# Sandwich layer on eight cores: LayerNorm sums through an accumulator output, one residual add on GpSimd, one PSUM copy on ScalarE

## The chip, the cores and the metric

One Trainium2 chip, all 8 cores, one program with different data on each core. The metric is device time in microseconds (us) of the slowest core. Engines are called PE (TensorE), DVE (VectorE), ACT (ScalarE), POOL (GpSimd) and SP (SyncE, which here only issues DMAs).

## What is computed

Input x is (2, 4096, 4096) float32. Each core has 1024 consecutive tokens of it (plus one neighbour row on each side for the convolution). Cut to what matters:

```python
def ln(x):   # no scale or shift; the last one of the layer has gamma and beta
    return (x - mean(x)) / sqrt(var(x) + 1e-5)

def attn(t1):
    c = conv1d(t1, conv_w, width 3, 4096 -> 3072) + conv_b
    q, k, v = split(c)                       # blocks of 128 tokens, 16 heads of 64
    o = softmax(causal(q wq . k wk / 8)) (v wv)
    return (o wo + bo) @ proj_w + proj_b      # -> a, (tokens, 4096)

def ffn(t2):
    h   = relu(t2 @ up_w) ** 2                 # 4096 -> 8192
    moe = (t2 @ fc1_w @ expert_w) * sum(top2(t2 @ gate_w))
    return ln(h @ down_w + moe @ fc2_w) * gamma + beta

x2  = x + ln(attn(ln(x)))
out = x2 + ln(ffn(ln(x2)))
```

## The kernel before

All weights stream from HBM; the matmuls use bf16. The work of a core goes through stages one after the other:

1. **First stage (lines 322 to 384), called A here.** 8 tiles of 128 tokens x 4096, then a ninth tile that holds the two halo rows. SP loads a tile of x (line 353). `ln_stats` (line 308) makes mean and 1/sigma: DVE sums the tile (`reduce_sum`), ACT squares it with an accumulator output beside that, then follow three DVE operations on one column and Ln and Exp on ACT. DVE normalizes to bf16 (line 360). `tm_to_fm` transposes in 8 groups: PE writes 4 transposes to one of two PSUM banks, DVE copies the group out (line 340), so that tokens lie along the columns.
2. Convolution (line 420), q, k and v, attention, output projections (line 670). The last one leaves the result feature-major in `a_fm`.
3. **Stage between projection and feed-forward (lines 692 to 765), called F here**, again 8 tiles of 128 tokens x 4096, one after the other:
   - SP loads x (line 706). PE transposes `a_fm` back in 8 groups (line 714), DVE copies each out to `atm` in bf16 (line 719).
   - `ln_stats` on `atm`, then DVE normalizes into `x2t`, float32 (line 729), and adds x in place (line 731). SP stores `x2t` (line 736).
   - `ln_stats` on `x2t`, DVE normalizes to `t2s`, bf16 (line 741). PE transposes (line 752), DVE copies to `stage` (line 756), SP stores it (line 761).
4. Feed-forward in two halves of 512 tokens; behind each half the final LayerNorm and the second residual add.

The work of each engine runs in the order in which the program is written. There is no scheduler: every wait is on a counting semaphore, and an engine that waits holds all that is behind it. SV counts DVE's operations, SC ACT's, SP (the semaphore) PE's groups, SX0 and SX1 loads of x, SS0 and SS1 stores. Each DVE and ACT operation goes through a wrapper (`EngWrap`) that first waits for the engine's own operation before, so all of them carry line 175. Three points on the order in stage F:

- The load of x for tile t+1 stands in SP's queue behind the store of tile t's `stage`, which waits for the last copy of tile t:

```python
        p.wait(sy, "SV", c_stage)                     # line 760, tile t
        ins = sy.dma_start(dt2sp[t], ...)
        p.wait(sy, "SV", xin_free[par])               # line 705, tile t+1
        c_load = p.inc(sy.dma_start(xinF[par], ...), f"SX{par}", 16)
```

- DVE waits for that load ahead of the sum over `atm` (line 722), though the sum does not read x.
- `stage` lies on `x2t`, so PE waits for the store of `x2t` (line 745) ahead of the second set of transposes.

Of the kernel before, what the change touches and what calls it, by code (L numbers as in the profile page):

```python
# [9 lines left out]
AF = mybir.ActivationFunctionType  # L10
ALU = mybir.AluOpType
# [4 lines left out]
D = 4096  # L16
# [11 lines left out]
EPS = 1e-5  # L28
# [98 lines left out]
class P:  # L127

    def __init__(self, nc):
        self.nc = nc  # L130
        self.sems = {}
        self.cnt = {}
        self._auto = set()
        names = ["SA", "SP", "SV", "SC", "SX0", "SX1", "SS0", "SS1",
                 "WQ", "WK", "WV", "WO"] + [f"D{i}" for i in range(5)]
        for name in names:
            self.sems[name] = nc.alloc_semaphore(name=name)
            self.cnt[name] = 0
# [44 lines left out]
def build(taps=(), stop_phase=99):  # L183
    nc = bass.Bass("TRN2", target_bir_lowering=False)
    p = P(nc)
    te, sy, po = nc.tensor, nc.sync, nc.gpsimd
    ve = EngWrap(p, nc.vector, "SV")
    se = EngWrap(p, nc.scalar, "SC")
# [65 lines left out]
    def stat(i):  # L254
        return stats[:, i : i + 1]
# [47 lines left out]
    def tap_barrier():  # L303
        if dtaps:
            for q in (te, sy, po, nc.vector, nc.scalar):
                p.wait(q, "SA")

    def ln_stats(src, sq_trash, width=D):
        p.inc(ve.reduce_sum(stat(S_SUM), src, axis=AX.X), "SV")
        ia = se.activation(sq_trash, src, AF.Square, accum_out=stat(S_SQ))  # L310
        c_sq = p.inc(ia, "SC")
        ve.tensor_scalar(stat(S_MU), stat(S_SUM), 1.0 / width, None, ALU.mult)
        p.wait(ve, "SC", c_sq)
        ve.tensor_tensor(stat(S_VAR), stat(S_MU), stat(S_MU), ALU.mult)
# [12 lines left out]
    t1s_free = [0, 0]
    tb_free = [0, 0]
# [15 lines left out]
    for t in range(NT + 1):  # L344
        par = t % 2
        if t == NT:
            p.wait(ve, "SV", xin_free[par])
            c = p.inc(ve.memset(xin[par], 0.0), "SV")
            p.wait(sy, "SV", c)
            ins = sy.dma_start(xin[par][0:2], dxh)  # L350
        else:
            p.wait(sy, "SV", xin_free[par])
            ins = sy.dma_start(xin[par], dx[t * 128 : (t + 1) * 128])
        c_load = p.inc(ins, f"SX{par}", 16)
        p.wait(ve, f"SX{par}", c_load)
        p.wait(se, f"SX{par}", c_load)
        p.wait(se, "SP", t1s_free[par])
        c_r = ln_stats(xin[par], t1s[par])
        p.wait(ve, "SC", c_r)
        iv = ve.tensor_scalar(t1s[par], xin[par], stat(S_MU), stat(S_R),  # L360
                              ALU.subtract, ALU.mult)
        c_n = p.inc(iv, "SV")
        xin_free[par] = c_n
        p.wait(te, "SV", c_n)
        if t < NT:
            tm_to_fm(t1s[par],
                     [t1T3[:, g * 4 : g * 4 + 4, 1 + t * 128 : 1 + (t + 1) * 128]
                      for g in range(8)])
        else:
            for g in range(8):  # L370
                tb = 4 + (g % 2)
                p.wait(te, "SV", tb_free[g % 2])
                for j in range(4):
                    ch = g * 4 + j
                    it = te.transpose(pbb[tb][:, j * 128 : (j + 1) * 128],
                                      t1s[par][:, ch * 128 : (ch + 1) * 128], id_bf)
                c = p.inc(it, "SP")
                p.wait(ve, "SP", c)
                src3 = pbb[tb].rearrange("p (a b) -> p a b", a=8)
                ve.tensor_copy(t1T3[:, g * 4 : g * 4 + 4, 0:1], src3[:, 0:4, 0:1])  # L380
                iv = ve.tensor_copy(t1T3[:, g * 4 : g * 4 + 4, 1025:1026], src3[:, 0:4, 1:2])
                tb_free[g % 2] = p.inc(iv, "SV")
        t1s_free[par] = p.cnt["SP"]
# [318 lines left out]
    p.wait(te, "SC", a_ready)  # L702
    for t in range(NT):
        par = t % 2
        p.wait(sy, "SV", xin_free[par])
        c_load = p.inc(sy.dma_start(xinF[par], dx[t * 128 : (t + 1) * 128]), f"SX{par}", 16)
        atm3 = atm[par].rearrange("p (a b) -> p a b", a=DC)
        p.wait(te, "SV", atm_free[par])
        for g in range(8):
            tb = 4 + (g % 2)  # L710
            p.wait(te, "SV", tb_free[g % 2])
            for j in range(4):
                m = g * 4 + j
                it = te.transpose(pbb[tb][:, j * 128 : (j + 1) * 128],  # L714
                                  a_fm[:, m * 1024 + t * 128 : m * 1024 + (t + 1) * 128],
                                  id_bf)
            c = p.inc(it, "SP")
            p.wait(ve, "SP", c)
            iv = ve.tensor_copy(atm3[:, g * 4 : g * 4 + 4],
                                pbb[tb].rearrange("p (a b) -> p a b", a=8)[:, 0:4])  # L720
            tb_free[g % 2] = p.inc(iv, "SV")
        p.wait(ve, f"SX{par}", c_load)
        p.wait(se, f"SS{par}", x2_spilled[par])
        p.wait(se, "SV", tb_free[0])
        p.wait(se, "SV", tb_free[1])
        c_r = ln_stats(atm[par], x2t[par])
        p.wait(ve, "SC", c_r)
        p.wait(ve, f"SS{par}", x2_spilled[par])
        ve.tensor_scalar(x2t[par], atm[par], stat(S_MU), stat(S_R),
                         ALU.subtract, ALU.mult)  # L730
        iv = ve.tensor_tensor(x2t[par], x2t[par], xinF[par], ALU.add)
        c_x2 = p.inc(iv, "SV")
        xin_free[par] = c_x2
        atm_free[par] = c_x2
        p.wait(sy, "SV", c_x2)
        c_spill = p.inc(sy.dma_start(dx2sp[t], x2t[par]), f"SS{par}", 16)
        p.wait(se, "SV", c_x2)
        p.wait(se, f"SS{par}", t2s_free[par])
        c_r2 = ln_stats(x2t[par], t2s[par])
        p.wait(ve, "SC", c_r2)  # L740
        iv = ve.tensor_scalar(t2s[par], x2t[par], stat(S_MU), stat(S_R),
                              ALU.subtract, ALU.mult)
        c_t2 = p.inc(iv, "SV")
        p.wait(te, "SV", c_t2)
        p.wait(te, f"SS{par}", c_spill)
        st3 = stage[par].rearrange("p (a b) -> p a b", a=DC)
        for g in range(8):
            tb = 4 + (g % 2)
            p.wait(te, "SV", tb_free[g % 2])
# [12 lines left out]
        t2s_free[par] = p.inc(ins, f"SS{par}", 16)
        x2_spilled[par] = t2s_free[par]
# [417 lines left out]
```

How the kernel before makes its waits and increments, by code:

```python
    def inc(self, instr, sem, n=1):  # L140
        if isinstance(instr, _Auto):
            return self.cnt[sem]
        instr.then_inc(self.sems[sem], n)
        self.cnt[sem] += n
        return self.cnt[sem]
# [1 line left out]
    def wait(self, eng, sem, val=None):  # L147
        v = self.cnt[sem] if val is None else val
        if v > 0:
            eng.wait_ge(self.sems[sem], v)
# [15 lines left out]
    def wait_ge(self, sem, v):  # L166
        return self._e.wait_ge(sem, v)
# [5 lines left out]
        def wrapped(*a, **k):  # L173
            p.wait(eng, semname)
            instr = fn(*a, **k)
            instr.then_inc(p.sems[semname], 1)
            p.cnt[semname] += 1
            return _Auto(instr)
```

## Time and profile before

| | us |
|---|---|
| two executions | 5212.37 and 4887.19, median 5049.78 |
| the profiled execution | 4884.38 |
| its span, first to last instruction, slowest core (core 3) | 4883.3 |
| spans of the eight cores | 4848.7 to 4883.3 |
| PE busy in the span | 3832.8 (78%) |
| DVE busy | 839.1 (17%) |
| ACT busy | 474.3 (10%) |
| POOL busy | 212.7 (4%) |

The profile is of the profiled execution on its slowest core. Busy shares are means over stages with different limits; what a stage waits for is read from its own stretch of the timeline and from the chain of waits that ended last. POOL is busy only with issuing DMAs.

### The profile page before, as it was taken

How to read it: one execution, taken by the hardware profiler on the slowest of the kernel's cores; microseconds unless marked ns; L12 is line 12 of the kernel's file. 1: busy time of each engine (PE TensorE's matmuls, PEld its weight loads, DVE VectorE, ACT ScalarE, POOL GpSimd, SP SyncE). 2: the span in 40 equal slices, each digit the busy share in tenths (PEclk: the TensorE clock that was granted, in tenths of full speed). 3: DMA queues.
4: the chain of work that ended last, by engine and by line, in shares of the span. 5: the costliest groups of instructions: out<-in, count | busy, mean ns of one | idle time of the engine just before them, and what ended most of it. 6: DMA issues, size and time to landing. Idle time of an engine off the chain costs nothing.

```text
span 4883.3 us, 43161 instructions; the slowest of 8 cores (4848.7 to 4883.3 us)
## 1 busy us (share of the span) xinstructions
PE 3832.8 (78%) x18161; PEld 1739.4 (36%) x18161; DVE 839.1 (17%) x1060; ACT 474.3 (10%) x621; POOL 212.7 (4%) x385
## 2 busy tenths in 40 slices
PE   1599999999648323879998999970779998999960
PEld 1244444444224111334443444430334443444430
DVE  4300000000360565110000000027110000000027
ACT  2100000002213221001111000001001111000001
POOL 0000000000001000000000000000000000000000
PEclk9999999999759655899999999985899999999985
DMA  6144444446004334568887777763569997777743
GB/s 157 38 75 75 75 76 78 78 78 104 0 1 60 113 129 150 101 114 153 152 152 137 142 134 140 144 128 117 112 122 151 154 153 137 134 140 143 139 91 116
DMA packets 76779, 548.38 MB, mean 112 GB/s; under 512 B 7529, under 2 KB 7977, under 8 KB 30506
## 3 DMA queue, kind: packets, MB, share of 16 engines
q0 software_dynamic: 64592, 444.69, 53.1%
q1 hardware_dynamic: 11998, 100.94, 5.8%
q8 instruction: 147, 2.41, 0.2%
q14 instruction: 42, 0.34, 0.0%
HBM read 948.32 MB, written 41.94 MB: 203 GB/s over the span
## 4 chain that ended last, share of the span: by engine, by line
PE 73%; DVE 13%; DMA 9%; issue 3%; SPq 1%; ACT 1%; DVEq 0%; ACTq 0%; POOL 0%; POOLq 0%
PE ps L902 21%; PE ps L420 20%; PE ps L1057 18%; DVE pool L175 13%; PE ps L995 5%; DMA pool<-fc1w 2%; PE ps L670 2%; DMA pool<-x 2%; PE ps L957 2%; DMA pool<-x2sp 1%; PE ps L489 1%; DMA pool<-expw 1%; SPq L831 1%; DMA pool<-fc2w 1%; ACT pool L175 1%
## 5 line engine op out<-in xcount | busy, mean ns | idle before, releaser
L902 PE MATMUL ps<-pool 128*128 128x512 bf16 x5120 | 1127.4, 383 | 55.0 <-DMA pool<-fc1w 36.2
L420 PE MATMUL ps<-pool 128*128 128x512 bf16 x4608 | 998.3, 379 | 0.9 <-DVE pool L175 0.9
L1057 PE MATMUL ps<-pool 128*128 128x512 bf16 x4096 | 899.4, 380 | 41.3 <-DMA pool<-fc2w 41.2
L902 PEld LDWEIGHTS ps<-pool 128*128 128x128 bf16 x5120 | 503.7, 99 | 680.7 <-issue 93.3
L175 DVE CAST pool<-ps 128x512 bf16<-128x512 f32 (+1 forms) x192 | 107.2, 558 | 3340.9 <-PE ps L995 1988.9
L420 PEld LDWEIGHTS ps<-pool 128*128 128x128 bf16 x4608 | 445.4, 97 | 553.6 <-issue 3.9
L1057 PEld LDWEIGHTS ps<-pool 128*128 128x128 bf16 x4096 | 397.4, 98 | 521.2 <-issue 49.4
L175 ACT ACTIVATE pool<-pool 128x512 bf16<-128x512 f32 (+5 forms) x259 | 260.9, 1007 | 1967.5 <-DVE pool L175 1934.1
L175 ACT ACTIVATE pool<-ps,pool 128x512 bf16<-128x512 f32 (+1 forms) x192 | 131.9, 687 | 1127.6 <-PE ps L420 975.1
L175 DVE TENSOR_REDUCE pool<-pool 128x1 f32<-128x4096 f32 (+2 forms) x73 | 220.3, 3018 | 81.7 <-DMA pool<-x 55.1
L995 PE MATMUL ps<-pool 128*128 128x512 bf16 x1024 | 231.5, 379 | 0.0
L752 PE MATMUL ps<-pool 128*128 128x128 bf16 x256 | 34.9, 302 | 234.6 <-DVE pool L175 234.6
L175 DVE COPY pool<-ps 128x128 bf16<-128x128 bf16 (+6 forms) x489 | 156.7, 320 | 328.1 <-PE ps L714 147.5
L175 DVE TENSOR_TENSOR pool<-pool 128x1 f32<-128x1 f32 (+3 forms) x106 | 188.5, 1779 | 63.5 <-DMA pool<-x2sp 52.5
L175 ACT ACTIVATE pool<-ps 128x512 f32<-128x512 f32 x128 | 76.4, 597 | 1246.7 <-PE ps L902 1246.7
L995 PEld LDWEIGHTS ps<-pool 128*128 128x128 bf16 x1024 | 100.1, 98 | 120.9
L957 PE MATMUL ps<-pool 128*128 128x512 bf16 x512 | 117.3, 391 | 21.9 <-DMA pool<-expw 19.4
L175 DVE TENSOR_SCALAR pool<-pool 128x1 f32<-128x1 f32 (+3 forms) x139 | 118.0, 849 | 46.6 <-ACT pool L175 35.8
L670 PE MATMUL ps<-pool 128*128 128x512 bf16 x512 | 113.5, 386 | 5.5 <-DMA pool<-projw 5.5
L867 PE MATMUL ps<-pool 128*1 128x128 f32 x8 | 3.0, 372 | 141.3 <-DVE pool L175 141.3
L752 PEld LDWEIGHTS ps<-pool 128*128 128x128 bf16 x256 | 22.9, 130 | 246.6 <-issue 246.6
L336 PE MATMUL ps<-pool 128*128 128x128 bf16 x256 | 35.0, 302 | 90.8 <-DVE pool L175 90.8
(59 smaller groups left out, 833.9 us busy)
## 6 DMA issues: line engine op xcount, KB each, us to landing
pool<-upw POOLq DMA_DIRECT2D x128, 1024.0 KB, 10.1
pool<-downw POOLq DMA_DIRECT2D x64, 2048.0 KB, 15.4
pool<-wconv POOLq DMA_DIRECT2D x72, 1024.0 KB, 16.4
pool<-x SPq DMA_DIRECT2D x16, 2048.0 KB, 10.9
pool<-fc1w POOLq DMA_DIRECT2D x32, 1024.0 KB, 9.3
pool<-fc2w POOLq DMA_DIRECT2D x32, 1024.0 KB, 19.4
x2sp<-pool SPq DMA_DIRECT2D x8, 2048.0 KB, 6.3
pool<-expw POOLq DMA_DIRECT2D x16, 1024.0 KB, 9.7
```

The lines of the kernel that those rows point to most:

```text
L175: instr = fn(*a, **k)
L336: it = te.transpose(pbb[tb][:, j * 128 : (j + 1) * 128], src_bf[:, ch * 128 : (ch + 1) * 128], id_bf)
L420: it = te.matmul(pbf[bk], sl[:, k * 128 : (k + 1) * 128], t1T[:, k * 1026 + base : k * 1026 + base + 512], start=(dw == 0 and k == 0), sto ...
L489: it = te.matmul(pbf[bk], w_sb[:, k * 1024 + pr * 128 : k * 1024 + (pr + 1) * 128], c_fm[:, (which * 8 + k) * 1024 + half * 512 : (which * ...
L670: it = te.matmul(pbf[bk], proj_sl[s][:, k * 128 : (k + 1) * 128], attnW[:, k * 1024 + half * 512 : k * 1024 + half * 512 + 512], start=(k ...
L752: it = te.transpose(pbb[tb][:, j * 128 : (j + 1) * 128], t2s[par][:, ch * 128 : (ch + 1) * 128], id_bf)
L831: ins = sy.dma_start(t2h3[:, :, tl * 128 : (tl + 1) * 128], dt2sp[half * 4 + tl])
L867: it = te.transpose(pbf[2][0:1, tl * 128 : (tl + 1) * 128], stat(S_RW), id_f32)
L902: it = te.matmul(pbf[bk], slots[s][:, k * 128 : (k + 1) * 128], rhs_fn(k), start=(k == 0), stop=(k == n_k - 1))
L957: it = te.matmul(pbf[bk], exp_sl[s][:, (j * LATC + k) * 128 : (j * LATC + k + 1) * 128], lat[:, k * 512 : (k + 1) * 512], start=(k == 0), ...
L995: it = te.matmul(pbf[bk], f2_sl[s][:, (j * LATC + k) * 128 : (j * LATC + k + 1) * 128], moe[:, k * 512 : (k + 1) * 512], start=False, stop ...
L1057: te.matmul(pbf[bk], dw_sl[s][:, k * 128 : (k + 1) * 128], hup[:, k * 512 : (k + 1) * 512], start=(k == 0), stop=False)
```

## The change

It has three parts, and the final LayerNorms keep the old `ln_stats`.

1. A new `ln_stats_fast` stands beside `ln_stats`. Instead of `reduce_sum`, DVE runs a `tensor_scalar` (times 1, plus 0) that writes the whole tile as float32 into a scratch area and puts the sum into `stat(S_SUM)` through the accumulator output. Stage A (9 calls) and stage F (16 calls) use it.
2. In stage F the 8 PSUM groups of the `a_fm` transposes are copied to `atm` by ACT (Identity) and no longer by DVE. PE waits for both kinds of copy (semaphores SC and SV) before each set of 8 groups.
3. In stage F the add `x2t + x` moves from DVE to POOL. A new semaphore SG carries its end to SP, PE, ACT and DVE.

```diff
+    def ln_stats_fast(src, sq_trash, sum_trash, width=D):
+        iv = ve.tensor_scalar(sum_trash, src, 1.0, 0.0, ALU.mult, ALU.add,
+                              accum_out=stat(S_SUM))
+        p.inc(iv, "SV")
+        ia = se.activation(sq_trash, src, AF.Square, accum_out=stat(S_SQ))
...
     def ln_stats(src, sq_trash, width=D):
         p.inc(ve.reduce_sum(stat(S_SUM), src, axis=AX.X), "SV")
...
-        c_r = ln_stats(xin[par], t1s[par])
+        c_r = ln_stats_fast(xin[par], t1s[par], trashA)
...
-        p.wait(te, "SV", atm_free[par])
+        p.wait(te, "SG", atm_free[par])
+        p.wait(te, "SV", tb_free2[0])
+        p.wait(te, "SV", tb_free2[1])
         for g in range(8):
             tb = 4 + (g % 2)
-            p.wait(te, "SV", tb_free[g % 2])
+            p.wait(te, "SC", af[g % 2])
...
-            p.wait(ve, "SP", c)
-            iv = ve.tensor_copy(atm3[:, g * 4 : g * 4 + 4],
-                                pbb[tb].rearrange("p (a b) -> p a b", a=8)[:, 0:4])
-            tb_free[g % 2] = p.inc(iv, "SV")
+            p.wait(se, "SP", c)
+            ia = se.activation(atm3[:, g * 4 : g * 4 + 4],
+                               pbb[tb].rearrange("p (a b) -> p a b", a=8)[:, 0:4],
+                               AF.Identity)
+            af[g % 2] = p.inc(ia, "SC")
         p.wait(ve, f"SX{par}", c_load)
         p.wait(se, f"SS{par}", x2_spilled[par])
-        p.wait(se, "SV", tb_free[0])
-        p.wait(se, "SV", tb_free[1])
-        c_r = ln_stats(atm[par], x2t[par])
+        p.wait(ve, "SC", af[0])
+        p.wait(ve, "SC", af[1])
+        c_r = ln_stats_fast(atm[par], x2t[par], trashF)
         p.wait(ve, "SC", c_r)
         p.wait(ve, f"SS{par}", x2_spilled[par])
-        ve.tensor_scalar(x2t[par], atm[par], stat(S_MU), stat(S_R),
-                         ALU.subtract, ALU.mult)
-        iv = ve.tensor_tensor(x2t[par], x2t[par], xinF[par], ALU.add)
-        c_x2 = p.inc(iv, "SV")
+        iv = ve.tensor_scalar(x2t[par], atm[par], stat(S_MU), stat(S_R),
+                              ALU.subtract, ALU.mult)
+        c_g = p.inc(iv, "SV")
+        p.wait(po, "SV", c_g)
+        p.wait(po, f"SX{par}", c_load)
+        it = po.tensor_tensor(x2t[par], x2t[par], xinF[par], ALU.add)
+        c_x2 = p.inc(it, "SG")
...
-        p.wait(sy, "SV", c_x2)
+        p.wait(sy, "SG", c_x2)
         c_spill = p.inc(sy.dma_start(dx2sp[t], x2t[par]), f"SS{par}", 16)
-        p.wait(se, "SV", c_x2)
+        p.wait(se, "SG", c_x2)
+        p.wait(ve, "SG", c_x2)
         p.wait(se, f"SS{par}", t2s_free[par])
-        c_r2 = ln_stats(x2t[par], t2s[par])
+        c_r2 = ln_stats_fast(x2t[par], t2s[par], trashF)
...
+        p.wait(te, "SC", af[0])
+        p.wait(te, "SC", af[1])
         for g in range(8):
             tb = 4 + (g % 2)
-            p.wait(te, "SV", tb_free[g % 2])
+            p.wait(te, "SV", tb_free2[g % 2])
```

How DVE's queue stands in stage F, the last tile (the semaphores each row waits for are in brackets; `ps` is PSUM, `pool` is SBUF, not the engine). Before:

```order
L175 COPY pool<-ps 128x512 [waits SP,SV] x16
L175 TENSOR_REDUCE pool<-pool 128x1 [waits SX1,SV]
L175 TENSOR_SCALAR pool<-pool 128x1 [waits SV]
L175 TENSOR_TENSOR pool<-pool 128x1 [waits SC,SV]
L175 TENSOR_SCALAR pool<-pool 128x1 [waits SV]
L175 TENSOR_SCALAR pool<-pool 128x4096 [waits SC,SS1,SV]
L175 TENSOR_TENSOR pool<-pool 128x4096 [waits SV]
L175 TENSOR_REDUCE pool<-pool 128x1 [waits SV]
```

After:

```order
L177 COPY pool<-ps 128x512 [waits SP,SV] x8
L177 TENSOR_SCALAR pool<-pool 128x4096 [waits SX1,SC,SV]
L177 TENSOR_SCALAR pool<-pool 128x1 [waits SV]
L177 TENSOR_TENSOR pool<-pool 128x1 [waits SC,SV]
L177 TENSOR_SCALAR pool<-pool 128x1 [waits SV]
L177 TENSOR_SCALAR pool<-pool 128x4096 [waits SC,SS1,SV]
L177 TENSOR_SCALAR pool<-pool 128x4096 [waits SG,SV]
```

Eight of the 16 copies and the full-width TENSOR_TENSOR have left DVE, both TENSOR_REDUCEs are TENSOR_SCALARs of 4096 columns, and the second one waits for POOL (SG) right behind the normalizing TENSOR_SCALAR.

POOL's queue at the same stage, after; before, nothing stood between the two DMA rows:

```order
L677 DMA pool<-projw 128x1024 [waits SP] x32
L759 TENSOR_TENSOR pool<-pool 128x4096 [waits SV,SX0]
L759 TENSOR_TENSOR pool<-pool 128x4096 [waits SV,SX1]
...
L759 TENSOR_TENSOR pool<-pool 128x4096 [waits SV,SX1]
L840 DMA pool<-gater 128x256 [waits SS0,SS1]
```

The 8 adds stand between the last projection weights and the first feed-forward weights, which wait for stage F's stores in both programs.

## Rows read from the trace of the kernel before

**Rows 1.** The page: the span, and the chain that ended last by engine.
```profile
span 4883.3 us, 43161 instructions; the slowest of 8 cores (4848.7 to 4883.3 us)
...
PE 73%; DVE 13%; DMA 9%; issue 3%; SPq 1%; ACT 1%; DVEq 0%; ACTq 0%; POOL 0%; POOLq 0%
```

**Rows 2.** Busy time by stretch: window length, then us (x instructions) of each engine, PEclk.
```profile
48.00:195.00 147.00, 45.54 (x308) 28.09 (x309) 99.83 (x126) 38.32 (x37) 0.00 (x0) 1.00 0.27 99
...
1611.00:1945.00 334.00, 81.44 (x528) 48.88 (x527) 211.60 (x222) 66.54 (x65) 1.59 (x3) 0.51 0.37 134
```

**Rows 3.** Timeline, first stage, tile 2: start us, us, engine, line, operation [idle before].
```profile
78.90 4.42 DVE L175 TENSOR_REDUCE pool<-pool 128x1 f32<-128x4096 f32 x1
...
84.98 2.41 DVE L175 TENSOR_SCALAR pool<-pool 128x4096 bf16<-128x4096 f32 x1 [0.82 <-ACT pool L175]
...
93.47 4.42 DVE L175 TENSOR_REDUCE pool<-pool 128x1 f32<-128x4096 f32 x1
```

**Rows 4.** Timeline, first stage: tile 0 (53 us) and the halo tile (174 us).
```profile
53.86 0.19 ACT L175 ACTIVATION_READ_ACCUMULATOR pool<-pool 128x1 f32 x1
54.22 0.16 DVE L175 TENSOR_TENSOR pool<-pool 128x1 f32<-128x1 f32 x1 [0.41 <-ACT pool L175]
...
177.55 0.19 ACT L175 ACTIVATION_READ_ACCUMULATOR pool<-pool 128x1 f32 x1
178.52 0.15 DVE L175 TENSOR_SCALAR pool<-pool 128x1 f32<-128x1 f32 x1
```

**Rows 5.** Timeline, stage between projection and feed-forward, tile 1.
```profile
1650.41 0.42 SPq L706 DMA_DIRECT2D pool<-x  x1
...
1650.87 0.95 DVE L175 COPY pool<-ps 128x512 bf16<-128x512 bf16 x2 [0.38 <-PE ps L714]
...
1652.19 0.95 DVE L175 COPY pool<-ps 128x512 bf16<-128x512 bf16 x2 [0.38 <-PE ps L714]
...
1655.43 3.62 ACT L175 ACTIVATE pool<-pool 128x4096 f32<-128x4096 bf16 x1 [14.55 <-DVE pool L175]
...
1662.66 4.42 DVE L175 TENSOR_REDUCE pool<-pool 128x1 f32<-128x4096 bf16 x1 [7.38 <-DMA pool<-x]
...
1668.75 2.41 DVE L175 TENSOR_SCALAR pool<-pool 128x4096 f32<-128x4096 bf16 x1 [0.82 <-ACT pool L175]
1671.26 4.43 DVE L175 TENSOR_TENSOR pool<-pool 128x4096 f32<-128x4096 f32 x1
...
1675.79 4.42 DVE L175 TENSOR_REDUCE pool<-pool 128x1 f32<-128x4096 f32 x1
1675.84 3.62 ACT L175 ACTIVATE pool<-pool 128x4096 bf16<-128x4096 f32 x1 [7.26 <-DVE pool L175]
1679.36 0.19 ACT L175 ACTIVATION_READ_ACCUMULATOR pool<-pool 128x1 f32 x1
1680.32 0.15 DVE L175 TENSOR_SCALAR pool<-pool 128x1 f32<-128x1 f32 x1
```

**Rows 6.** Groups of that stage by form: count | busy us, mean ns | idle before.
```profile
L175 DVE COPY pool<-ps 128x512 bf16<-128x512 bf16 x128 | 54.3, 424 | 172.6 <-PE ps L714 147.5 <-PE ps L752 18.1 <-DVE pool L175 0.5
L175 DVE TENSOR_TENSOR pool<-pool 128x4096 f32<-128x4096 f32 x8 | 35.4, 4424 | 0.8
...
L175 DVE TENSOR_REDUCE pool<-pool 128x1 f32<-128x4096 bf16 x8 | 35.4, 4420 | 46.8 <-DMA pool<-x 46.8
...
L175 DVE TENSOR_SCALAR pool<-pool 128x4096 f32<-128x4096 bf16 x8 | 19.3, 2412 | 7.0 <-ACT pool L175 7.0
```

**Rows 7.** Chain that ended last, same stage: the shortest x load.
```profile
1846.74 9.96 DMA pool<-x
```

**Rows 8.** ScalarE's groups by form, whole program.
```profile
L175 ACT ACTIVATE pool<-ps,pool 128x512 bf16<-128x512 f32 x128 | 88.1, 688 | 1073.4 <-PE ps L420 975.1 <-PE ps L670 75.0 <-PE ps L533 22.3
...
L175 ACT ACTIVATE pool<-ps 128x512 f32<-128x512 f32 x128 | 76.4, 597 | 1246.7 <-PE ps L902 1246.7
```

**Rows 9.** The page's DMA issues: KB each, median us to landing.
```profile
x2sp<-pool SPq DMA_DIRECT2D x8, 2048.0 KB, 6.3
```

More of the change, by code:

```diff
@@ L78 @@
 RE_PROJSL = 176256
+RF_TRASH = 176256
+RA_TRASH = 168064
 N_PROJSL = 4
@@ L133, in __init__ @@
         self._auto = set()
-        names = ["SA", "SP", "SV", "SC", "SX0", "SX1", "SS0", "SS1",
+        names = ["SA", "SP", "SV", "SC", "SG", "SX0", "SX1", "SS0", "SS1",
                  "WQ", "WK", "WV", "WO"] + [f"D{i}" for i in range(5)]
@@ L306, in tap_barrier @@
                 p.wait(q, "SA")
+    def ln_stats_fast(src, sq_trash, sum_trash, width=D):
[3 more added lines that the diff above has]
+        ia = se.activation(sq_trash, src, AF.Square, accum_out=stat(S_SQ))
+        c_sq = p.inc(ia, "SC")
+        ve.tensor_scalar(stat(S_MU), stat(S_SUM), 1.0 / width, None, ALU.mult)
+        p.wait(ve, "SC", c_sq)
+        ve.tensor_tensor(stat(S_VAR), stat(S_MU), stat(S_MU), ALU.mult)
+        iv = ve.tensor_scalar(stat(S_VAR), stat(S_SQ), 1.0 / width, stat(S_VAR),
+                              ALU.mult, ALU.subtract)
+        c_v = p.inc(iv, "SV")
+        p.wait(se, "SV", c_v)
+        se.activation(stat(S_R), stat(S_VAR), AF.Ln, bias=EPS, scale=1.0)
+        return p.inc(se.activation(stat(S_R), stat(S_R), AF.Exp, bias=0.0, scale=-0.5), "SC")
     def ln_stats(src, sq_trash, width=D):
@@ L323, in build @@
     t1T3 = t1T.rearrange("p (k c) -> p k c", k=DC)
+    trashA = bF(RA_TRASH, D)
     xin = [bF(RA_XIN0, D), bF(RA_XIN1, D)]
@@ L696, in build @@
     t2s = [bB(RF_T2S0, D), bB(RF_T2S1, D)]
+    trashF = bF(RF_TRASH, D)
+    af = [0, 0]
+    tb_free2 = [0, 0]
     xin_free = [0, 0]
@@ L704, in build @@
         par = t % 2
-        p.wait(sy, "SV", xin_free[par])
+        p.wait(sy, "SG", xin_free[par])
         c_load = p.inc(sy.dma_start(xinF[par], dx[t * 128 : (t + 1) * 128]), f"SX{par}", 16)
         atm3 = atm[par].rearrange("p (a b) -> p a b", a=DC)
-        p.wait(te, "SV", atm_free[par])
+        p.wait(te, "SG", atm_free[par])
+        p.wait(te, "SV", tb_free2[0])
+        p.wait(te, "SV", tb_free2[1])
         for g in range(8):
             tb = 4 + (g % 2)
-            p.wait(te, "SV", tb_free[g % 2])
+            p.wait(te, "SC", af[g % 2])
             for j in range(4):
@@ L757, in build @@
                                 pbb[tb].rearrange("p (a b) -> p a b", a=8)[:, 0:4])
-            tb_free[g % 2] = p.inc(iv, "SV")
+            tb_free2[g % 2] = p.inc(iv, "SV")
         c_stage = p.cnt["SV"]
@@ L835, in build @@
     load_t2(0)
+    tb_free[0] = tb_free[1] = p.cnt["SV"]
     for half in range(2):
```

## The prediction

> **What bounds the kernel now.** I read the page first: in the chain that ended last PE has 73%, DVE 13%, DMA 9% [rows 1]. PE's share lies in the convolution, the projections and the feed-forward, which the change does not touch. DVE's and DMA's shares lie in the stages between them, so I cut those out by time: stage A runs for some 147 us with DVE busy 99.83, stage F for some 334 us with DVE busy 211.60 and ACT 66.54 [rows 2]. Two thirds busy is not a full engine, so the timeline has to say what holds the rest.
>
> In stage A one tile follows the other in a single chain. From the sum of tile 2 to the sum of tile 3 it is 93.47 - 78.90 = 14.57 us: sum 4.42, column operations and Ln and Exp to 84.98, normalizing 2.41, then transposes and copies, and the next sum at once [rows 3]. The loads are early. So every microsecond of the sum is on the path, except in two tiles where ACT's square ends as late as or shortly behind the sum [rows 4].
>
> In stage F the chain goes through a transfer. The last copy of a tile lets SP store it and issue the next load of x, 1650.41; the load is waited for until 1662.66, where DVE has been idle for 7.38 us; then sum 4.42, normalizing 2.41, add 4.43, second sum at 1675.79 [rows 5]. All 8 first sums wait for x, 46.8 us in total [rows 6]. The transposes of `a_fm` and their copies run inside that wait. What comes behind the load is serial.
>
> **The change part by part.** The sum is made against the profiled execution: span 4883.3, whole 4884.38, so 1.1 us lie around the span. The median of the two runs shown, 5049.78, is the middle of two values 6.7% apart (4887.19 and 5212.37). The profiled execution agrees with the lower one, and my forecast is for such executions.
>
> *The copies on ACT: 0.* Nothing in the trace shows ACT copying bf16 out of PSUM at this shape; the nearest rows of 128x512 from PSUM take 0.597 us without and 0.688 us with a second operand, against 0.424 for DVE [rows 8, 6]. Two groups on two banks took 1652.19 - 1650.87 = 1.32 us on DVE [rows 5]. With the longer ACT row a pair takes 1.32 + 0.26 = 1.58, 8 groups 6.3. PE may also start the set only when DVE has finished the last two copies of the tile before, some 0.7 later than now. Together `atm` is ready about 7.3 us behind the last `stage` copy, where the load lands 0.4 + 9.96 = 10.4 us behind it at the soonest [rows 5, 7]. Cover of 3 us is left. ACT's square follows (3.62 + 0.1), to 11.1, and is needed only when the sum is done, at 14.9. DVE gets rid of 64 copies, but it stood idle for x anyway: no gain. If the cover were gone, the price would be 7.3 - 5.3 = 2 us a tile, 16 in all.
>
> *The add on POOL: +35.4.* Behind the add, DVE, ACT, PE and SP all need `x2t`, so nothing runs beside it. DVE's 4.42 us goes [rows 6] and POOL's time comes. The trace has no arithmetic on POOL. Below, POOL can hardly beat DVE, which takes 4.42 both for two inputs and for one input into a sum, so one element per step whatever is read: that bound is +0. Above, I take an engine that makes three passes for each element, two reads and a write one after the other: 3 x 4.42 = 13.3 us, +70.8. I take the middle, two passes for the two inputs, 2 x 4.42 = 8.84: 8 x (8.84 - 4.42) = +35.4. That choice is an estimate, and the largest uncertain term.
> The Trainium skill (GPSIMD Engine Reference, section 3.1) has a measured price: 4497 ns against 2293 ns for a float32 add of 2048 elements, since two inputs share GpSimd's one read path. The trace agrees on the DVE side (4.42 us at 4096); taken twice, 4497 ns makes about 9.0 us and this term +36.6.
>
> *New hand-overs: +0.8.* Two same-engine steps of 0.1 us (normalizing ends 1671.16, add starts 1671.26 [rows 5]) become DVE to POOL and POOL to DVE. Other crossings in the chain cost 0.17 (ACT's accumulator read ends 54.05, DVE starts 54.22 [rows 4]). I take +0.1 a tile; 0.5 per crossing would be the far end, +6.4 in all.
>
> *The new sum: +2.4.* This is the part that could bring most. The trace has no DVE operation with an accumulator output. Below, it runs like the normalizing TENSOR_SCALAR of the same width, 2.41 us, which is 0.59 ns per element [rows 3, 6]. Above, it runs like the reduce, 4.42, which is 1.08 ns per element, the same for bf16 and float32 input [rows 3, 6]. Both read one tile; what sets them apart is that the reduce puts every element into one running total, and the new form does so too. I take the reduce's time. The sum must also be fetched: ACT has its own row for that, which begins 0.1 us before the square ends and adds 0.1 net [rows 5]. 24 of 25 calls lie on the path (tile 0 of stage A waits for ACT): 24 x 0.1 = +2.4; with a whole small DVE row of 0.15 and its gap, 0.26 [rows 5], it would be +6.2. Writing the tile into scratch is beside the reading and costs nothing, as the normalizing row, which also writes it, shows.
> The Trainium skill speaks against this part as well (SBUF — State Buffer, section Who interferes with whom): it excepts the `tensor_scalar` that also writes out its accumulator from the operations that may use both port pairs. No row here shows that form. By the rule this term stays at about +2.4.
>
> *What stays.* The wait for x ahead of the first sum stays, and so does SP's order. The store of `x2t` now leaves when POOL is done and lands 6.3 us later [rows 9], while another sum and normalizing, 4.42 + 2.41 = 6.8 us alone, stand between the add and the second transposes: still hidden. POOL's queue holds no DMA that is wanted in stage F. The conv, attention and feed-forward code is the same, the renamed waits included.
>
> Sum: +35.4 + 0.8 + 2.4 = +38.6. Span 4883.3 + 38.6 = 4921.9, and with the 1.1 around it **4923.0 us**, 0.8% slower than the profiled execution. About 2% (98 us) is what a measurement can tell from no change, so this counts as within it.
>
> **The rivals.**
> *A. Not slower: the accumulating sum runs at the rate of TENSOR_SCALAR.* Its place is the 25 sums. Price: tiles 1 to 7 of stage A gain 2.01 each, 14.1. The halo tile gains only until ACT's square holds it, 177.74 + 0.17 against 178.52 + 0.26 = 178.78 for the column operation that needs it: 0.9 [rows 4]. Stage F's first sums gain 8 x 2.01 = 16.1, as the square started inside the wait for x. Its second sums start together with the square, which ends at 1679.55, so the next column operation that needs it comes at 1679.72 in place of 1680.32 + 0.26 = 1680.58: 0.86 x 8 = 6.9 [rows 5]. Together -38.0, and with the other terms +0.6: 4885.0. It decides from a sum of about 2.5 us. For it speaks that the instruction has the same name as the 2.41 us row; against it, that a running total is the very thing the 4.42 us rows have in common.
> The Trainium skill's tier table (VectorE: DVE Perf Modes, section The perf-mode tier table) gives `tensor_scalar` on float32 twice the rate and names no exception; taken by its letter it would make this case. The rows bear out its two rates (2.41 and 4.42), not which of them the new form has.
> *B. POOL's add costs three passes, 13.3 us.* +70.7 + 0.8 + 2.4 = +73.9: 4958.3. Nothing in the profile excludes it. Slower by over 2% it becomes only above 4.4 + (98 - 3.2)/8 = 16.3 us per add.
> *C. POOL adds as fast as DVE*: +3.2, 4887.6. An add is independent per element, but two inputs through a narrower engine speak against it.
> *D. The ACT copies outlast the load*: +16 on top, 4939. Against it: 3 us of cover even by the longer row. An ACT copy would need 1.1 us.
>
> **How the numbers follow.** Forecast 0.70 (own range 4905 to 4940: POOL 7.5 to 9.5 us, hand-overs and reads at their far ends). A 0.14, B 0.07, C 0.04, D 0.02, an add above 16.3 us 0.03. The range of 8 in 10 takes in A and B: 4884 to 4960. Faster by over 2% would need 98 us, where A and C together with nothing lost give some 35 at most: 0.01 for what I do not see. Slower by over 2%: 0.04. Within: 0.95.
>
> **What would show it.** In stage A: the sum row at 4.42 us with a short accumulator read behind it, and 14.6 to 14.7 us from tile to tile; at 2.4 the step is 12.6 and A holds. In stage F: POOL rows of 8.8 us between DVE's normalizing and the second sum; each tile 4.7 us longer from x load to x load; DVE still idle for x ahead of the first sum, and ACT's copies ended before that. If DVE's first sum is released by ACT in place of the DMA, D holds. The forecast is wrong if stage F grows by under 25 or over 55 us, if stage A moves by more than 3, or if anything else moves by more than 10.

## The result, and the profile after

The changed kernel takes 4927.0 us (median of 11), the one before, run beside it, 4891.52 (median of 10). The ratio is 1.0077, 95% interval 1.0065 to 1.0089: slower by 0.8%. In some executions of either kernel the four cores of one die show a lower granted clock (0.83 in place of 0.90 in the one of 5286.23 us); one such made the median of the first two runs 5049.78, and the ratio leaves them out. The profiled execution took 4922.84 us against 4884.38, +38.5, where +38.6 was forecast.

The page of the kernel after: its span, the busy time by engine and the chain that ended last.

```profile
span 4921.8 us, 43228 instructions; the slowest of 8 cores (4892.2 to 4921.8 us)
...
PE 3828.3 (78%) x18161; PEld 1739.3 (35%) x18161; DVE 776.8 (16%) x1013; ACT 512.4 (10%) x685; POOL 283.2 (6%) x393
...
PE 73%; DVE 12%; DMA 9%; issue 3%; POOL 1%; ACT 1%; SPq 1%; DVEq 0%; ACTq 0%; POOLq 0%
```

Against [rows 1], DVE has lost a point of the chain and POOL has one. In the busy time POOL has gone from 212.7 to 283.2 and DVE from 839.1 to 776.8. DVE does less, and the kernel is slower: the copies left DVE where it was waiting anyway, and the add went to POOL where everything waits for it.

Where the time came from is read off two stretches. In what follows stage F is measured from the issue of its first load of x to the issue of its last store of `stage`, on every core, and the figure is the mean of the eight: 307.2 us before, 346.3 after, +39.1. In this measure one core of the same kernel differs from another by up to 9 us, so the mean is worth more than the slowest core, and a difference of 2 us between two such means is not clear of scatter.

Stage A after, tile 2 (timeline: start us, us, engine, line, operation):

```profile
78.69 4.42 DVE L177 TENSOR_SCALAR_CACHE_REDUCE pool<-pool 128x4096 f32<-128x4096 f32 x1
83.03 0.08 DVE L177 DVE_READ_ACCUMULATOR pool<-pool 128x1 f32 x1
83.22 0.15 DVE L177 TENSOR_SCALAR pool<-pool 128x1 f32<-128x1 f32 x1
...
84.78 2.41 DVE L177 TENSOR_SCALAR pool<-pool 128x4096 bf16<-128x4096 f32 x1 [0.82 <-ACT pool L177]
...
93.29 4.42 DVE L177 TENSOR_SCALAR_CACHE_REDUCE pool<-pool 128x4096 f32<-128x4096 f32 x1
```

It answers to [rows 3]. The sum has a new name and the old duration, 4.42 us; its fetch takes 0.08 us and begins before the sum's row ends. From sum to next column operation it is 83.22 - 78.69 = 4.53 us, against 83.42 - 78.90 = 4.52. The step from tile to tile is 93.29 - 78.69 = 14.60 us, against 14.57: a call costs 0.03 us more.

DVE's groups by form, the whole program, say the same of all 25 calls (count | busy us, mean ns | idle before and what ended it):

```profile
L177 DVE TENSOR_SCALAR_CACHE_REDUCE pool<-pool 128x4096 f32<-128x4096 f32 x17 | 75.1, 4420 | 84.5 <-POOL pool L759 73.6 <-DMA pool<-x 7.0 <-DMA pool<-xhalo 3.2
...
L177 DVE TENSOR_SCALAR_CACHE_REDUCE pool<-pool 128x4096 f32<-128x4096 bf16 x8 | 35.4, 4420 | 220.9 <-DMA pool<-x 199.6 <-ACT pool L177 21.3
...
L177 DVE DVE_READ_ACCUMULATOR pool<-pool 128x1 f32 x25 | 2.1, 83 | 0.0
```

Stage F after, tile 1, from the load of x on:

```profile
1654.14 0.42 SPq L728 DMA_DIRECT2D pool<-x  x1
1654.68 1.29 ACT L177 ACTIVATE pool<-ps 128x512 bf16<-128x512 bf16 x2 [9.74 <-PE ps L738]
...
1659.12 1.29 ACT L177 ACTIVATE pool<-ps 128x512 bf16<-128x512 bf16 x2 [0.19 <-PE ps L738]
1660.50 3.62 ACT L177 ACTIVATE pool<-pool 128x4096 f32<-128x4096 bf16 x1
1664.02 0.19 ACT L177 ACTIVATION_READ_ACCUMULATOR pool<-pool 128x1 f32 x1
1664.29 4.42 DVE L177 TENSOR_SCALAR_CACHE_REDUCE pool<-pool 128x4096 f32<-128x4096 bf16 x1 [10.60 <-ACT pool L177]
1668.63 0.08 DVE L177 DVE_READ_ACCUMULATOR pool<-pool 128x1 f32 x1
...
1670.38 2.41 DVE L177 TENSOR_SCALAR pool<-pool 128x4096 f32<-128x4096 bf16 x1 [0.82 <-ACT pool L177]
1672.99 8.80 POOL L759 TENSOR_TENSOR pool<-pool 128x4096 f32<-128x4096 f32 x1 [34.16 <-DVE pool L177]
...
1681.98 4.42 DVE L177 TENSOR_SCALAR_CACHE_REDUCE pool<-pool 128x4096 f32<-128x4096 f32 x1 [9.20 <-POOL pool L759]
...
1688.08 2.41 DVE L177 TENSOR_SCALAR pool<-pool 128x4096 bf16<-128x4096 f32 x1 [0.82 <-ACT pool L177]
...
1691.10 1.01 PE L783 MATMUL ps<-pool 128*128 128x128 bf16 x8 [31.44 <-DVE pool L177]
```

It answers to [rows 5]. The add is 8.80 us on POOL, in a gap of DVE that nothing fills (normalizing ends 1672.79, second sum starts 1681.98). The ACT copies run from 1654.68 to 1660.41 inside the wait for x. The sum at 1664.29 follows the end of ACT's accumulator read at 1664.21, and the profile names ACT as its releaser in two of the eight tiles. That is a trap: by the code the sum waits for ACT's copies and the load, not for the square, and the copies ended at least 2.2 us before the sum in all 64 tiles of the eight cores. Tile 3 shows it:

```profile
1746.86 3.62 ACT L177 ACTIVATE pool<-pool 128x4096 f32<-128x4096 bf16 x1
1750.06 4.42 DVE L177 TENSOR_SCALAR_CACHE_REDUCE pool<-pool 128x4096 f32<-128x4096 bf16 x1 [10.01 <-DMA pool<-x]
1750.38 0.19 ACT L177 ACTIVATION_READ_ACCUMULATOR pool<-pool 128x1 f32 x1
```

Here the sum begins while the square is still running. It was the load each time, which happened to land near the square's end: in every odd tile, the ones whose landing the trace holds, the sum starts 0.31 to 0.67 us behind it. (The 0.67 is tile 1, on all eight cores; in the run with the new sum alone the last tile has such 0.35 us more, with the square long done. What they are stays open.)

### The profile page after: what moved, and what is told of

The parts are those of the page before. It is cut to its first block, busy times and chain, and to the rows that moved or that the text cites. A ratio compares the mean times of both kernels' runs of the same rounds, so it can differ in the third digit from the quotient of the medians.

```text
span 4921.8 us, 43228 instructions; the slowest of 8 cores (4892.2 to 4921.8 us)
## 1 busy us (share of the span) xinstructions
PE 3828.3 (78%) x18161; PEld 1739.3 (35%) x18161; DVE 776.8 (16%) x1013; ACT 512.4 (10%) x685; POOL 283.2 (6%) x393
## 4 chain that ended last, share of the span: by engine, by line
PE 73%; DVE 12%; DMA 9%; issue 3%; POOL 1%; ACT 1%; SPq 1%; DVEq 0%; ACTq 0%; POOLq 0%
PE ps L934 21%; PE ps L439 20%; PE ps L1089 18%; DVE pool L177 12%; PE ps L1027 5%; DMA pool<-fc1w 3%; PE ps L689 2%; PE ps L989 1%; POOL pool L759 1%; DMA pool<-x 1%; DMA pool<-x2sp 1%; PE ps L508 1%; DMA pool<-expw 1%; ACT pool L177 1%; DMA pool<-fc2w 1%
## 5 line engine op out<-in xcount | busy, mean ns | idle before, releaser
L177 ACT ACTIVATE pool<-ps 128x512 f32<-128x512 f32 (+1 forms) x192 | 114.6, 597 | 1324.0 <-PE ps L934 1246.6
L783 PE MATMUL ps<-pool 128*128 128x128 bf16 x256 | 34.9, 302 | 259.4 <-DVE pool L177 259.4
L177 DVE TENSOR_TENSOR pool<-pool 128x1 f32<-128x1 f32 (+3 forms) x98 | 153.1, 1563 | 62.0 <-DMA pool<-x2sp 51.9
L177 DVE TENSOR_SCALAR_CACHE_REDUCE pool<-pool 128x4096 f32<-128x4096 f32 (+1 forms) x25 | 110.5, 4420 | 305.5 <-DMA pool<-x 206.6
L177 DVE COPY pool<-ps 128x128 bf16<-128x128 bf16 (+6 forms) x425 | 129.6, 305 | 178.5 <-PE ps L1047 52.3
L920 POOL DMA_DIRECT2D pool<-upw x128 | 67.7, 529 | 832.6 <-PE ps L934 786.0
L177 DVE TENSOR_REDUCE pool<-pool 128x1 f32<-128x8 f32 (+4 forms) x48 | 109.9, 2289 | 22.5 <-ACT pool L177 18.2
```

Source lines behind the costliest of these rows:

```text
L177: instr = fn(*a, **k)
L783: it = te.transpose(pbb[tb][:, j * 128 : (j + 1) * 128], t2s[par][:, ch * 128 : (ch + 1) * 128], id_bf)
L920: ready[m] = (dsem[s], p.inc(po.dma_start(slots[s], dram_fn(m)), dsem[s], 16))
```

## The experiments

**The parts one by one.** Three runs put one part each on the kernel before, a fourth takes POOL's part out of the kernel after.

The accumulating sum alone, and with a bf16 scratch output:

```diff
-        p.inc(ve.reduce_sum(stat(S_SUM), src, axis=AX.X), "SV")
+        iv = ve.tensor_scalar(sum_trash, src, 1.0, 0.0, ALU.mult, ALU.add,
+                              accum_out=stat(S_SUM))
```

> Before, with the accumulating sum alone (25 calls). Theory (the running total takes elements one at a time, fetch is short): sum rows 4.42 us, an accumulator read of 0.08 us behind each, stage A 14.60 us per tile against 14.57, stage F within 1.5 us of before, whole time +0 to +2 us. Rival (the sum is faster where no other part of the change stands beside it): sum rows near 2.4 us and -38 us.

Measured: ratio 0.9983 (0.9963 to 1.0004), stage F 306.8 us (-0.4), stage A 14.60 us a tile. No gain, and a loss of 0.03 us a tile that neither stage F nor the whole time can show.

> The accumulating sum alone on before, with the scratch output in bf16: the second input to the choice of rate (bf16 in and bf16 out in the first sum of stage F, float32 in and bf16 out in the others). Theory (the running total sets one element per step whatever the types): all rows 4.42 us. Rival (a narrower output or bf16 on both sides lets it run faster): 2.4 us or less for the bf16 rows.

Groups by form in stage F of that run:

```profile
L177 DVE TENSOR_SCALAR_CACHE_REDUCE pool<-pool 128x4096 bf16<-128x4096 f32 x8 | 35.4, 4420 | 1.0
L177 DVE TENSOR_SCALAR_CACHE_REDUCE pool<-pool 128x4096 bf16<-128x4096 bf16 x8 | 35.4, 4420 | 42.1 <-DMA pool<-x 42.1
```

All 4420 ns, bf16 to bf16 too. The rate of the form does not depend on the types tried, so rival A does not hold for these either. The Trainium skill's exception for this form (SBUF — State Buffer, section Who interferes with whom) agrees with these rows; its tier table (VectorE: DVE Perf Modes, section The perf-mode tier table), read without that exception, does not. (One execution: 4881.36 us.)

The copies on ACT alone:

```diff
-            p.wait(ve, "SP", c)
-            iv = ve.tensor_copy(atm3[:, g * 4 : g * 4 + 4], ...)
+            p.wait(se, "SP", c)
+            ia = se.activation(atm3[:, g * 4 : g * 4 + 4], ..., AF.Identity)
...
+        p.wait(te, "SC", af[0])
+        p.wait(te, "SC", af[1])
```

> Before, with the 64 copies of the first transposes on ACT alone, PE's waits as in the change. Theory (hidden under the load of x): stage F -1 to +3 us, where the up to 3 us are PE's longer start ahead of the second transposes (0.25 us a tile); DVE waits for x ahead of the first sum in every tile. Rival (the copies are on the path): stage F +16 us, DVE released by ACT.

Measured: ratio 1.0014 (0.9997 to 1.0031), stage F 308.9 us (+1.7). Groups by form:

```profile
L177 ACT ACTIVATE pool<-ps 128x512 bf16<-128x512 bf16 x64 | 38.2, 597 | 77.3 <-PE ps L738 74.2
...
L177 DVE TENSOR_REDUCE pool<-pool 128x1 f32<-128x4096 bf16 x8 | 35.4, 4420 | 222.6 <-DMA pool<-x 222.6
```

ACT takes 0.597 us for a group where DVE took 0.424 [rows 6], and DVE's idle time ahead of the first sums (144 us of the 222.6 lie ahead of the first tile, in the projection) is ended by the load of x in all eight tiles. What the 1.7 us hold is small waits. PE starts the second transposes 0.57 us behind the normalizing (1685.03 to 1685.60) where before it took 0.36; over all 64 tiles the means are 0.57 and 0.375. Its queue now has two waits for ACT's semaphore there, 0.106 us each. And where the landing of x is in the trace, the first sum starts 0.30 us behind it in place of 0.16, with two waits for ACT's semaphore more in DVE's queue, 0.07 us each. Together that is 0.34 us a tile, 2.7 in all, which agrees with the +1.7 within the scatter of the means.

The add on POOL alone, and the kernel after with the add back on DVE:

```diff
-        iv = ve.tensor_tensor(x2t[par], x2t[par], xinF[par], ALU.add)
-        c_x2 = p.inc(iv, "SV")
...
+        it = po.tensor_tensor(x2t[par], x2t[par], xinF[par], ALU.add)
+        c_x2 = p.inc(it, "SG")
```

> Before, with the add on POOL alone. Theory (the add is serial, POOL takes 8.80 us against 4.43 and two hand-overs 0.2 us more): stage F +8 x 4.6 = +37 us, whole time about +37 us (0.75%). Rival (the loss comes from the parts together, as DVE and POOL share something when both work): under +25 us here, and POOL's rows shorter than 8.8 us.

> The changed kernel with the add back on DVE and nothing else undone. Theory: stage F falls from 346 us to 308 to 311 us, whole time 0 to +3 us against before. Rival (parts together): more than a third of the +36 us stays.

Measured, alone: 4918.63 us in the profiled execution, stage F 344.2 us (+37.0). There is no interval for it. Undone: ratio 1.0010 (0.9992 to 1.0028), stage F 309.3 us (+2.1 against before). So the parts add up, -0.4 + 1.7 + 37.0 = +38.3 against +39.1 for all, and a loss by their joint working, the rival, is at most the 0.8 us between the two, which is within scatter. Groups by form in stage F, POOL alone:

```profile
L734 POOL TENSOR_TENSOR pool<-pool 128x4096 f32<-128x4096 f32 x8 | 70.4, 8801 | 274.5 <-DVE pool L175 274.5
...
L175 DVE TENSOR_REDUCE pool<-pool 128x1 f32<-128x4096 bf16 x8 | 35.4, 4420 | 44.5 <-DMA pool<-x 44.5
L175 DVE TENSOR_REDUCE pool<-pool 128x1 f32<-128x4096 f32 x8 | 35.4, 4420 | 73.4 <-POOL pool L734 73.4
```

The 73.4 us of DVE idle time ahead of the second sums are new. That is 9.2 us a tile: POOL's 8.80 and two hand-overs of 0.2.

**Why DVE's relief was worth nothing.** If the load of x covers the first copies, taking it away must both gain time and expose what ACT's copies cost.

```diff
     for t in range(NT):
         par = t % 2
+        load_x(t + 1)
...
-        p.wait(ve, f"SX{par}", c_load)
...
         c_r = ln_stats(atm[par], x2t[par])
...
+        p.wait(ve, f"SX{par}", c_load)
         iv = ve.tensor_tensor(x2t[par], x2t[par], xinF[par], ALU.add)
```

> Before, with the load of x issued one tile ahead and waited for only in front of the add; all else as before. Theory (stage F is bound by the load that hides the first copies, 10.8 us from the last stage copy to the sum against 5.4 us for transposes and copies): each tile 5 to 5.5 us shorter, stage F 307 - 42 = 265 us, whole time -0.8 to -0.9%. Rival (transfers or DVE's other waits take the time anyway): stage F less than 15 us shorter.

> As the run with the early load, but with the first copies on ACT, so that nothing hides them. Theory (the copies cost nothing in the change only because the load covers them): 1.4 us a tile for the slower copies and the later start, 0.2 for the hand-over and 0.25 for PE's longer start, so stage F 12 to 18 us longer than with the early load alone, whole time +0.3% against it. Rival (DVE freed of 64 copies gains something once the load is out of the way): stage F equal or shorter.

Measured: early load 0.9913 (0.9892 to 0.9935), stage F 266.2 us, where 265 was expected. Early load with ACT copies 0.9958 (0.9941 to 0.9976), stage F 279.3 us, +13.1. Timeline of the early load, tile 1:

```profile
1647.24 0.55 SPq L709 DMA_DIRECT2D pool<-x  x1
...
1651.64 0.42 DVE L175 COPY pool<-ps 128x512 bf16<-128x512 bf16 x1 [0.37 <-PE ps L724]
1652.17 4.42 DVE L175 TENSOR_REDUCE pool<-pool 128x1 f32<-128x4096 bf16 x1
...
1660.77 4.43 DVE L175 TENSOR_TENSOR pool<-pool 128x4096 f32<-128x4096 f32 x1
```

The sum starts 0.1 us behind the last copy; the load of x for the tile after is just on its way. The 5 us or so a tile that DVE "waited for the load" were real and free to take. In this order the ACT copies cost 13.1/8 = 1.6 us a tile, PE's and DVE's further waits included: rival D's price, seen once its cover is gone.

**Whether DVE and POOL can add together.** The add cut by columns (NV is 2752):

```diff
+        it = po.tensor_tensor(x2t[par][:, NV:D], x2t[par][:, NV:D], xinF[par][:, NV:D], ALU.add)
+        c_pg = p.inc(it, "SG")
+        iv = ve.tensor_tensor(x2t[par][:, 0:NV], x2t[par][:, 0:NV], xinF[par][:, 0:NV], ALU.add)
```

> Before, with the add cut by columns: DVE takes 2752, POOL 1344, both at once. Theory P (DVE and POOL share a read path, so one waits for the other): rows of 2.97 us on DVE and 2.89 us on POOL laid end to end, or both stretched to the sum, 5.9 to 6.1 us in all against 4.43, stage F +12 us. Theory Q (they are independent): both rows as long as alone and beside each other, 3.1 us and a hand-over of 0.2, stage F -8 us.

Measured: 1.0025 (1.0011 to 1.0039), stage F 320.7 us, +13.5. Timeline, tile 0:

```profile
1630.50 3.02 DVE L175 TENSOR_TENSOR pool<-pool 128x2752 f32<-128x2752 f32 x1
1630.60 5.79 POOL L737 TENSOR_TENSOR pool<-pool 128x1344 f32<-128x1344 f32 x1 [30.84 <-DVE pool L175]
...
1636.56 4.42 DVE L175 TENSOR_REDUCE pool<-pool 128x1 f32<-128x4096 f32 x1 [3.04 <-POOL pool L737]
```

DVE takes its 3.02 us. POOL, which starts 0.1 us later, has a row of 5.79 us for 1344 columns. At 8.80/4096 = 2.15 ns per column they take 2.89, an estimate; the other 2.90 are what was left of DVE's row when POOL began (2.92). In the first two tiles of all eight cores POOL's row is 5.78 to 5.80 us. So theory P holds: with two SBUF inputs each, the two adds take as long as one after the other, and it was POOL, second to start, that waited. The Trainium skill (SBUF — State Buffer, section Who interferes with whom) says that a DVE instruction with two SBUF inputs contends with a GpSimd one that reads SBUF, and the trace agrees to 0.1 us.

**An order in which the two moves pay.** In the next runs PE and ACT make the first copies of tile t+1 while DVE works on tile t, and x is loaded early. The sums are plain again, and ACT's squares write into the scratch area. `a_trans` is transposes and ACT copies, `ln1` the first LayerNorm and the add, `ln2` the second with transposes and store:

```diff
+    for t in range(NT):
+        load_x(t + 1)
+        ln1(t)
+        spill(t)
+        a_trans(t + 1)
...
+        ln2(t)
```

> Stage F reordered: load of x one tile ahead, ACT makes the first copies of tile t+1 while DVE normalizes and adds tile t, plain sums, add on DVE. Theory (the ACT copies pay only where they are made beside DVE's work on another tile): a tile takes 33.4 - 5.35 = 28.1 us, stage F 231 us, whole time -1.5 to -1.7% against before. Rival (the copies delay ACT's second square): stage F over 245 us.

> The same order with the add on POOL, in its old place between the two LayerNorms of one tile. Theory: 4.6 us a tile more, as it stands alone on the path: stage F +37 us against the add on DVE, 268 us. Rival (with DVE relieved the add hides in part): under +25 us.

Measured with the add on DVE: 0.9846 (0.9825 to 0.9867), stage F 232.1 us against 231 expected. With the add on POOL in the same place: 4849.0 us in the profiled execution, stage F 268.6 us, +36.4. So ACT's copies do pay once they stand beside DVE's work on another tile. POOL's add costs the same 4.6 us a tile in a stage that is 75 us shorter: it stays serial whatever is around it. Groups by form, add on DVE:

```profile
L177 ACT ACTIVATE pool<-ps 128x512 bf16<-128x512 bf16 x64 | 38.2, 598 | 9.4 <-PE ps L749 5.4 <-ACT pool L177 0.4
...
L177 DVE TENSOR_REDUCE pool<-pool 128x1 f32<-128x4096 bf16 x8 | 35.4, 4420 | 143.2 <-ACT pool L177 142.5
```

(The 142.5 us ahead of the first sums are the wait of the first tile again. ACT now stands idle for PE ahead of these copies for 5.4 us in all, against 74.2 in the run with ACT's copies and nothing else.)

Then DVE does `ln1(t + 1)`, whose add is on POOL, before `ln2(t)`, so that POOL adds tile t+1 beside `ln2(t)`. Groups 4 to 8 of `a_trans(t + 2)` stand inside `ln2(t)`, behind its Ln and Exp:

```diff
+    for t in range(NT):
+        ln1(t + 1)
+        spill(t)
+        load_x(t + 2)
+        a_trans(t + 2, 0, 4)
+        ln2(t)
```

> The add on POOL with other work beside it: DVE does the first LayerNorm of tile t+1 before the second of tile t, so POOL adds tile t+1 while DVE does the second LayerNorm of tile t. Theory (8.8 us on POOL are free when hidden, but DVE's 2.41 us normalizing does not run beside POOL's reads): 26.5 us a tile, stage F about 224 us, 0.1% faster than with the add on DVE. Rival 1 (no sharing): 23.4 us a tile, stage F 199 us. Rival 2 (order too tight, ACT's copies late): above 231 us.

Measured: 4810.1 us in the profiled execution, stage F 228.8 us. That is 3.3 us less than with the add on DVE (232.1), and 4.8 more than the theory's 224: neither the theory nor a rival foresaw what the timeline shows. Timeline, one tile:

```profile
1701.04 4.42 DVE L177 TENSOR_REDUCE pool<-pool 128x1 f32<-128x4096 f32 x1
1701.14 8.87 POOL L779 TENSOR_TENSOR pool<-pool 128x4096 f32<-128x4096 f32 x1 [18.72 <-DVE pool L177]
...
1705.57 0.15 DVE L177 TENSOR_SCALAR pool<-pool 128x1 f32<-128x1 f32 x1
1705.83 4.20 DVE L177 TENSOR_TENSOR pool<-pool 128x1 f32<-128x1 f32 x1
...
1711.17 2.41 DVE L177 TENSOR_SCALAR pool<-pool 128x4096 bf16<-128x4096 f32 x1 [0.82 <-ACT pool L177]
```

The row of 4.20 us is the square of the mean, one column of 128 values, 0.16 us elsewhere [rows 4]. It ends at 1710.03, and POOL's add at 1701.14 + 8.87 = 1710.01. A two-input DVE operation on a single column is held for POOL's whole remaining add; on all eight cores, each of the 64 such rows that meet POOL's add ends 0.01 to 0.03 us behind it. I had looked for the lock on the normalizing pass and not on that row.

```diff
-        ve.tensor_tensor(stat(S_VAR), stat(S_MU), stat(S_MU), ALU.mult)
+        ve.tensor_scalar(stat(S_VAR), stat(S_MU), stat(S_MU), None, ALU.mult)
```

> As the run with POOL's add hidden, but the square of the mean (128x1) is a TENSOR_SCALAR with one tensor input and a column as scalar, in place of a TENSOR_TENSOR with two SBUF inputs, which took 4.17 to 4.20 us there and ended with POOL's add. Theory T1 (a two-input DVE operation waits for POOL's reads, and so does the 2.41 us normalizing): the small row 0.16 us, the normalizing now waits or is stretched until POOL ends, 1.1 us a tile gained, stage F about 220 us, -1.8% against before. Theory T2 (only two-input operations wait): normalizing 2.41 us at once beside POOL, 3.9 us a tile gained, stage F about 198 us, -2.2%. Rival (the 4.2 us had another cause): no change from 229 us.

Measured: 4799.25 us in the profiled execution against 4884.38 of the kernel before, -1.7%, without an interval. Stage F 218.6 us. Timeline, one tile:

```profile
1690.75 2.41 DVE L177 TENSOR_SCALAR pool<-pool 128x4096 f32<-128x4096 bf16 x1 [0.89 <-ACT pool L177]
...
1693.27 4.42 DVE L177 TENSOR_REDUCE pool<-pool 128x1 f32<-128x4096 f32 x1
1693.37 8.85 POOL L793 TENSOR_TENSOR pool<-pool 128x4096 f32<-128x4096 f32 x1 [17.36 <-DVE pool L177]
...
1697.79 0.80 DVE L177 TENSOR_SCALAR pool<-pool 128x1 f32<-128x1 f32 x3
...
1699.41 4.96 DVE L177 TENSOR_SCALAR pool<-pool 128x4096 bf16<-128x4096 f32 x1 [0.82 <-ACT pool L177]
```

The three column operations take 0.80 us together, beside POOL. The normalizing pass, 2.41 us at 1690.75 where POOL is idle, takes 4.96 at 1699.41, where POOL adds until 1702.22: it ends 2.15 us behind POOL's end, and so it is in all 56 tiles of the eight cores where it meets POOL's add. So it was held as well, as T1 has it, and its wait is 2.5 us in place of the 4.0 of the small row. Stage F is 10.2 us shorter, 1.3 a tile, and T2's 198 us is excluded. The Trainium skill (same page and section) has this rule too, that a DVE pass in a two-port mode and GpSimd exclude each other and the first to issue goes first; the timeline agrees, POOL's row of 8.85 us is as long as beside the plain sum and DVE's is the one that grew. This is the fastest version: 88.6 us off stage F of before, of which 41 are the early load, 34 the ACT copies in the shadow of DVE, 13.5 the last two steps together. Those two also have another order of DVE's work, which was not tried with the add on DVE, so how much of the 13.5 is POOL's is not shown.

## What the prediction had right, and which steps failed

The forecast, 4923.0 us, met the profiled execution (4922.84) and the median (4927.0), and the mechanism of the loss is the one it gave: POOL's add stands alone on the path, the copies ran under the load. But two of its terms were wrong, in opposite directions: the price of the new sum, +2.4 where +0.7 was measured, and the renamed waits, which it put at nothing and which cost 2.7. That the total met to 0.2 us is luck.

- *The new sum: +2.4.* This step failed in size. The rate was right (4.42 us in all 25 rows, whatever the types). The fetch, taken from ACT's accumulator read as 0.1 us net, is a row of 0.08 us that lies within the end of the sum's. A call costs 0.03 us from tile to tile (14.57 to 14.60), 0.7 for the 24 on the path. Alone, the new sum changed stage F by -0.4 us, less than cores differ.
- *What stays: the renamed waits at nothing.* This step failed too; no reason was given for it. From the end of the second normalizing to PE's second transposes it is 0.572 us on the mean of 64 tiles, 0.375 before: PE's queue has two more waits there, for ACT's semaphore, 0.106 us each. DVE has two more ahead of the first sum, 0.07 us each, behind the load that ends its wait. The first came with ACT's copies alone as well (0.57), and not with POOL's add alone (0.37). Together 0.34 us a tile, +2.7 in all. I did not read those gaps before.
- *Copies on ACT: 0.* Right about the cover. ACT's copy takes 0.597 us, the shorter of the two rows named, `atm` is ready 6.7 us behind the last `stage` copy (7.3 forecast), and the load ends the wait in every tile. The cover itself was read from one core's chain: its shortest load is 9.96 us, but on the eight cores before the first sum starts as soon as 8.7 us behind the load's issue. The price without cover was named as 2 us a tile, measured 1.6.
- *The add on POOL: +35.4.* Measured 8 x (8.801 - 4.425) = +35.0, from a row of 8.80 where 8.84 was taken. That value was twice DVE's row, chosen between bounds of 4.4 and 13.3, and no row of the trace before supported it more than that; the price in the Trainium skill (GPSIMD Engine Reference, section 3.1), doubled to 9.0, was 0.2 over. The value was good, the reasoning from rows was thin, and this largest term came out by a choice.
- *Hand-overs: +0.8.* Too small: 1672.79 to 1672.99 and 1681.79 to 1681.98 are 0.39 us in place of 0.2, +1.5 in all. By the 0.17 us a crossing that the prediction itself read, it should have been 8 x 2 x 0.07 = +1.1.
- With the measured sizes the terms of stage F are 35.0 + 1.5 + 0.2 + 2.7 = +39.4 (0.2 is the fetch, 16 calls at 0.01 us; the other 0.02 us a call lie in the gap ahead of the sum, which the hand-over row holds); stage F grew by 39.1.
- The sentence that a measurement tells about 2% from no change was too coarse. Some ten executions a side gave an interval of 0.24%, so the 0.8% that the forecast named is a loss clear of noise, and to count it as within no change was a mistake. The chance of 0.95 for within 2% was right as stated.
- The base: the two runs shown before had a median of 5049.78, all ten together 4891.5. Against that first median the forecast would read as 2.5% faster; working from the profiled execution was what made it usable.
- Rival A (a sum at 2.4 us) fell by the rows and by the run with bf16; B and C by the row of 8.80; D by the load, which ended the wait in every tile, though the profile names ACT in two, which the prediction had given as the sign of D.

## What to carry to other kernels

Before taking work off an engine, look at what ends its idle time ahead of that work: here DVE's copies ran under a load, so moving them gained nothing until the load was issued a tile earlier (-0.9%) and the copies stood beside another tile's work (-1.5% with both). A slower engine is free only where its result is not waited for; an add moved to POOL between two steps of one chain costs its whole extra time, every tile. And an instruction's name does not give its rate: a TENSOR_SCALAR that also accumulates ran at the reduce's rate. Each further semaphore that an engine waits for has a price too, small but paid every tile. Whether the sum would be cheaper on another engine or beside another tile's work was not tried.

## What the runs showed of the hardware

- DVE's TENSOR_SCALAR with an accumulator output shows as TENSOR_SCALAR_CACHE_REDUCE, 4.42 us for 4096 columns for f32 and bf16 on either side, against 2.41 without the output, and is followed by DVE_READ_ACCUMULATOR, 0.08 us, which overlaps its end.
- POOL's float32 add of 128x4096 takes 8.80 us, very steadily (70.4 us for 8), and 8.82 to 8.87 where DVE works beside it.
- The hold between DVE and POOL does not care for size. A two-input operation on one column waited 4.0 us for POOL's add (a row of 4.20 in place of 0.16), the one-input normalizing of 4096 columns waited 2.5 us, both to within 0.3 us of POOL's end; in the split add it was POOL that waited, for DVE, which had started 0.1 us before it. One-input operations on a column (0.15 to 0.21 us) and the plain sum (4.42) were not held. The held time is inside the row of the waiting instruction, so it looks like a slow instruction and not like a wait.
- A further semaphore to wait for costs time even when it was reached long ago: 0.106 us each in PE's queue (0.36 to 0.57 us for two, from the end of DVE's pass to the first matmul), 0.07 us each in DVE's (0.16 to 0.30 us for two, from the landing of x to the sum).
